# A perceiver layer on one core: FFN weight differences move from cross attention to self attention, and cross attention is reordered

## The reference, cut to what matters

```python
x = x + xattn(layernorm(x), ctx, Wq_d, W_qk, Wkv_d, Wv_u)       # 8 batches, 64 queries, 16 heads, 1601 context rows
x = x + attn(layernorm(x), ..., k_cache, v_cache, block_idx)     # 32 heads of 128, 8 key groups, 512 + 64 keys
x = x + ffn(layernorm(x), w1, mean_w1, w2, mean_w2, w3, mean_w3)

def xattn(Q, K, ...):
    C_kv = K @ Wkv_d                                             # 1601 x 32 per batch
    scores = ((Q @ Wq_d @ W_qk) per head) @ C_kv.T / sqrt(32)
    return softmax(scores) @ (C_kv @ Wv_u per head)

def weight(w, base):                                             # ffn: for w1, w3, w2
    d = w - base
    return base + mean(abs(d)) * sign(d)
h = silu(x @ W1.T) * (x @ W3.T);  y = h @ W2.T                   # inner size 1792
```

## Time and profile before

| | |
|---|---|
| three runs | 907.76, 906.02, 902.95 us; median 906.02 |
| profiled execution | 903.59 us, span 901.8 us |
| PE, DVE, ACT, POOL busy | 96%, 68%, 58%, 46% of the span |
| mean granted PE clock | 0.987 of full |
| cross attention | to 287 us (first score of batch 0 at 45 us) |
| keys and values of self attention | 287 to 316 us |
| heads of self attention | 316 to 764 us; grouped outputs begin 56.2 us apart (435.92, 492.15, 548.38) |
| output, norm and FFN | 764 to 902 us |
| ACT idle before exponentials of cross attention, ended by POOL's sums | 6.4 us in 3 waits |

### The profile page before, as it was taken

The page is one execution under the profiler, slowest core; times in us unless marked ns, Lnnn a source line. Parts: engine busy times, 40 slices in busy tenths (PEclk is TensorE's granted clock), DMA queues, the critical chain, the costliest instruction groups (busy, mean ns, idle before and its releaser), DMA issues.

```text
span 901.8 us, 15515 instructions
## 1 busy us (share of the span) xinstructions
PE 861.6 (96%) x5402; PEld 654.4 (73%) x5402; DVE 609.3 (68%) x994; ACT 521.6 (58%) x1011; POOL 416.4 (46%) x272
## 2 busy tenths in 40 slices
PE   6899999999987979999999999999999999899998
PEld 4445555555532768888888888888888887788886
DVE  4865676577543448768587685876858769767784
ACT  4756666666675546546365463654636557555552
POOL 2597787778874024423244232442324525144430
PEclk9989999999998989999999999999999999999999
DMA  9947756532651522011020110201102004446521
GB/s 358 325 169 273 275 209 213 192 127 66 217 174 59 222 83 71 24 41 54 0 70 23 43 50 0 70 23 40 53 0 70 13 1 137 144 141 204 188 99 47
DMA packets 43202, 102.96 MB, mean 114 GB/s; under 512 B 7954, under 2 KB 13074, under 8 KB 42258
## 3 DMA queue, kind: packets, MB, share of 16 engines
q1 hardware_dynamic: 42866, 102.06, 33.0%
q10 hardware_dynamic: 288, 0.26, 0.1%
HBM read 96.95 MB, written 1.05 MB: 109 GB/s over the span
## 4 chain that ended last, share of the span: by engine, by line
PE 61%; DVE 2%; ACT 1%; DMA 1%; POOL 0%; SPq 0%; issue 0%
PE psum L1359 11%; PE psum L1345 10%; PE psum L1475 9%; PE psum L1413 8%; PE psum L1371 6%; PE psum L1489 4%; PE psum L1398 3%; PE psum L1389 3%; PE psum L1394 3%; PE psum L1380 1%; PE psum L1392 1%; PE psum L1390 1%; DMA ffn_raw<-in_L_ffn_mean_w_dram 1%; POOL ffn_quant L1860 0%; DVE x L1831 0%; DVE norm_stats L162 0%
## 5 line engine op out<-in xcount | busy, mean ns | idle before, releaser
L1847 POOL TENSOR_TENSOR head_probs<-head_probs,inverse_den 128x576 f32<-128x576 f32 x128 | 147.4, 1152 | 273.1 <-DVE inverse_den L1700 273.0
L982 DVE TENSOR_REDUCE max_part<-psum 128x1 f32<-128x804 f32 x128 | 121.0, 989 | 44.0 <-PE psum L694 43.9
L871 ACT ACTIVATE probs<-psum 128x512 f32<-128x512 f32 (+1 forms) x208 | 107.9, 601 | 54.7 <-PE psum L715 48.1
L1582 ACT ACTIVATE head_probs<-psum,neg_max 128x576 f32<-128x576 f32 x128 | 94.8, 741 | 51.1 <-DVE neg_max L1713 50.4
L555 POOL TENSOR_TENSOR prob_sums<-probs 128x1024 f32<-128x1024 f32 x48 | 114.2, 2389 | 18.7 <-ACT probs L871 9.8
L1713 DVE TENSOR_REDUCE neg_max<-psum 128x1 f32<-128x576 f32 x128 | 96.9, 757 | 23.8 <-PE psum L1359 22.6
L1359 PE MATMUL psum<-k_high,query_t_high 128*128 (+1 forms) x256 | 86.6, 338 | 2.0 <-DVE coeff L1786 2.0
L1693 DVE TENSOR_TENSOR probs_t_low<-psum,probs_t_high 128x512 fp32r<-128x512 f32 x124 | 84.8, 684 | 1.0
L715 PE MATMUL psum<-q_t,c_t 97*128 97x512 f32 (+1 forms) x208 | 73.7, 435 | 7.9 <-ACT probs L871 6.3
L1371 PE MATMUL psum<-ident,head_probs 128*128 128x128 f32 x496 | 77.9, 273 | 1.6 <-DVE query_t_low L1672 1.4
L694 PEld LDWEIGHTS psum<-c_t,q_t 96*128 96x128 f32 x256 | 43.6, 190 | 47.9 <-DVE max_part L982 25.1
(11 more groups left out here) (221 smaller groups left out, 1919.3 us busy)
## 6 DMA issues: line engine op xcount, KB each, us to landing
ctx_t_odd<-in_ctx_dram SPq DMA_DIRECT2D x4, 3202.0 KB, 10.7
w_raw<-in_L_ffn_w_dram SPq DMA_DIRECT2D x24, 448.0 KB, 5.1
w_raw<-in_L_ffn_mean_w_dram SPq DMA_DIRECT2D x24, 448.0 KB, 6.4
ffn_raw<-in_L_ffn_w_dram SPq DMA_DIRECT2D x42, 256.0 KB, 3.8
ffn_raw<-in_L_ffn_mean_w_dram SPq DMA_DIRECT2D x42, 256.0 KB, 4.3
cache<-in_ctx_dram SPq DMA_DIRECT2D x3, 3202.0 KB, 10.8
wq_nat<-in_L_attn_wq_dram SPq DMA_DIRECT2D x32, 256.0 KB, 3.0
wo_nat<-in_L_attn_wo_dram SPq DMA_DIRECT2D x32, 256.0 KB, 2.7
```

The lines of the kernel that those rows point to most:

```text
L871: act.activation(prob_buffer(b, t)[0:rows, half * BANK:(half + 1) * BANK], psum[0:rows, n % SCORE_BANKS, :], ACT.Exp, scale=XSCALE).then_i ...
L982: dve.tensor_reduce(max_part[:, qt, pair:pair + 1], psum[:, bank:bank + 2, 0:PIECE_KEYS], AX.XY, ALU.max).then_inc(s_max, 1)
L1582: act.activation(probs[:, qt, :].rearrange("p (a k) -> p a k", a=2), psum[:, 2 * (qt % 2):2 * (qt % 2) + 2, 0:HALF], ACT.Exp, bias=neg_max ...
L1847: pool.tensor_tensor(probs[:, qt, :], probs[:, qt, :], rden[:, qt:qt + 1].to_broadcast([P, KEYS]), ALU.mult).then_inc(s["norm"], 1)
```

## The change

In `cross_attention`: the pieces of the FFN weights, their loads, differences and sums are taken out. The ring has 8 probability buffers. `values` takes two units at a visit, three visits a batch. POOL adds tiles into fewer sums (`GROUPED`): three for batches 0 to 4, five for 5 and 6, seven (two of them a single tile) for 7; tiles are added one by one, 10, 8 and 6 additions a batch (7 before). The values of the last, short tile go into the first pass of the denominators, and that function stands directly behind `turn_max`, ahead of `natural` and the next batch's first scores; before, the denominators stood behind those scores. Maxima and scores alternate one by one.

In `attention_and_ffn`: the pieces are 1024 wide, 7 of them, one per group from the second on. SP loads the three pairs (six DMAs of 512 KB) in its loop, after the wait for ACT's sum of the group before. POOL subtracts behind `values(g)` in the first head, ACT sums behind `output_weight_high(g, 0)`, POOL adds to the total in the second head. Two of the piece buffers lie over the selected keys, dead by then. The coefficient is made in the third head of the last group. `difference(0)` moves ahead of POOL's first head.

```diff
 def cross_attention
+STEADY = ((0, 1, 2, 3), (4, 5, 6, 7), (8, 9, 10, 11, 12))
+FEWER = ((0, 1, 2), (3, 4, 5), (6, 7), (8, 9), (10, 11, 12))
+FEWEST = ((0, 1, 2), (3, 4), (5, 6), (7, 8), (9, 10), (11,), (12,))
+GROUPED = (STEADY,) * (BATCH - 3) + (FEWER, FEWER, FEWEST)
+RING, SUMS = 8, 6
...
 max_scores, i == 1:
                     pe.wait_ge(s_d, 2 * (b - 1))
+                    if b + 1 < BATCH:
+                        pe.wait_ge(s_cnat, b + 2)
...
+            def tail_and_denominators(b):
...
                 if b + 3 < BATCH:
-                    pe.wait_ge(s_cnat, b + 4)
+                    pe.wait_ge(s_cp, b + 4)
                 elif b + 1 < BATCH:
                     pe.wait_ge(s_max, MAXIMA * (b + 2) - 1)
...
+                pe.wait_ge(s_exp, HALVES * (b + 1))
+                pe.wait_ge(s_add, adds_through(b, parts[0][-1]))
+                for half in range(2):
+                    at = 2 * LKV * half
+                    mm = pe.matmul(psum[at:at + LKV, U_BANK, :], c_nat[0:TAIL, b % 3, KT - 1, :],
+                                   prob_buffer(b, KT - 1)[0:TAIL, half * BANK:(half + 1) * BANK], start=False, stop=True)
+                    add_up(0, 1, half)
+                mm.then_inc(s_pv, 1)
+                for n in range(1, len(parts), 2):
+                    wait(pe, s_add, adds_through(b, parts[n + 1][-1]))
                     for half in range(2):
+                        add_up(n, 0, half)
+                        mm = add_up(n + 1, 1, half)
                 mm.then_inc(s_den, 1)
...
 PE's loop over batches:
+                maximum(0)
+                scores(b, 2)
+                if b == 0:
+                    maximum(1)
+                    compress(2)
+                scores(b, 3)
+                if b > 0:
+                    maximum(1)
+                    mix(b - 1)
+                maximum(2)
+                if b == 0:
+                    natural(2)
+                scores(b, 4)
+                maximum(3)
+                scores(b, 5)
+                maximum(4)
+                values(b, range(0, 2))
+                for t in range(6, 10):
+                    maximum(t - 1)
+                    scores(b, t)
+                maximum(9)
+                values(b, range(2, 4))
+                for t in range(10, KT):
+                    maximum(t)
+                    scores(b, t)
+                maximum(KT)
+                values(b, range(4, 6))
+                maximum(KT + 1)
+                maximum(KT + 2)
                 if b + 3 < BATCH:
                     compress(b + 3)
                 if lead:
                     turn_max(b + 1)
-                values(b, UNITS - 1)
+                tail_and_denominators(b)
                 if b + 3 < BATCH:
                     natural(b + 3)
                 if lead:
                     scores(b + 1, 0)
                     scores(b + 1, 1)
-                denominators(b)
...
 ACT's loop over batches:
-                    if t == ABS_AT:
-                        abs_sum(b, 0)
...
-                abs_sum(b, 1)
-                abs_sum(b, 2)
...
 attention_and_ffn, SP's loop:
+                    if i == 1:
+                        sp.wait_ge(s_abs, 3 * (g - 1) + 1)
+                        for k in range(3):
+                            for j, n in enumerate(wnames[k]):
+                                sp.dma_start(pieces[k][:, j, :], flat[n][:, bass.ds((g - 1) * PIECE, PIECE)]
+                                             ).then_inc(s_piece[k], 16)
...
 PE, score:
+                if isinstance(g, int) and n == NH - 2 and qt == 1:
+                    pe.wait_ge(s_tot, NKV)
+                    pe.matmul(psum[:, 3, HALF:HALF + 3], ones[:, :], total[:, :], start=True, stop=True).then_inc(s_all, 1)
+                elif isinstance(g, int) and n == NH - 2 and qt == 3:
+                    pe.wait_ge(s_co, 1)
...
 PE, start:
-            pe.wait_ge(s_ones, 1)
-            pe.wait_ge(s_tot, 1)
-            pe.matmul(psum[:, 7, 0:3], ones[:, :], total[:, :], start=True, stop=True).then_inc(s_all, 1)
-            pe.wait_ge(s_co, 1)
...
 ACT, head:
                 if this and i == 0:
                     output_weight_high(g, i)
+                if last and i == 0:
+                    for k in range(3):
+                        abs_sum(g, k)
+
+            def abs_sum(g, k):
+
+                if k == 0:
+                    act.wait_ge(s_tot, g)
+                act.wait_ge(s_pdiff, 3 * (g - 1) + k + 1)
+                act.activation(pieces[k][:, 0, :], pieces[k][:, 0, :], ACT.Abs,
+                               accum_out=part[:, k:k + 1]).then_inc(s_abs, 1)
...
 POOL, head:
+                if i == 1 and last and not (isinstance(g, int) and g == 0):
+                    pool.wait_ge(s_abs, 3 * g + 1)
+                    pool.tensor_tensor(total[:, :], total[:, :], part[:, :], ALU.add).then_inc(s_tot, 1)
                 if i == 0:
                     wait(pool, s["pv"], n)
                     values(g)
-                if isinstance(g, int) and (g, i) == (NKV - 1, 0):
-                    difference(0)
+                if i == 0 and last:
+                    pool.wait_ge(s["vl"], 2 * g + 2)
+                    for k in range(3):
+                        pool.wait_ge(s_piece[k], 32 * g)
+                        pool.tensor_tensor(pieces[k][:, 0, :], pieces[k][:, 0, :], pieces[k][:, 1, :],
+                                           ALU.subtract).then_inc(s_pdiff, 1)
...
 POOL, start:
+            pool.wait_ge(s["wql"], 2)
+            difference(0)
             run(pool, head)
```

More of the change, by code:

```diff
@@ L327, with adds_of, adds_before, adds_through @@
 C_WIDTH = MAIN + TAIL
-DIFF_AT = (0, 1, 2)
-ABS_AT = 3
+STEADY = ((0, 1, 2, 3), (4, 5, 6, 7), (8, 9, 10, 11, 12))
+FEWER = ((0, 1, 2), (3, 4, 5), (6, 7), (8, 9), (10, 11, 12))
+FEWEST = ((0, 1, 2), (3, 4), (5, 6), (7, 8), (9, 10), (11,), (12,))
+GROUPED = (STEADY,) * (BATCH - 3) + (FEWER, FEWER, FEWEST)
+def adds_of(b):
+    return [(t, n, t == tiles[1]) for n, tiles in enumerate(GROUPED[b]) for t in tiles[1:]]
+def adds_before(b):
+    return sum(len(adds_of(i)) for i in range(b))
+def adds_through(b, t):
+    done = [i + 1 for i, (at, n, first) in enumerate(adds_of(b)) if t == at or (first and t == GROUPED[b][n][0])]
+    return adds_before(b) + done[0] if done else 0
+def sum_number(b, n):
+    return sum(1 for i in range(b) for tiles in GROUPED[i] if len(tiles) > 1) + n
 COMPRESS_BANK = (4, 3, 6) + (4,) * (BATCH - 3)
@@ L440, in cross_attention, with tile_before, visits_done, tile_summed @@
     s_x = core.sem("x_updated", own)
-    wnames = (("w1", "mean_w1"), ("w3", "mean_w3"), ("w2", "mean_w2"))
-    flat = {n: arg[n].rearrange("r c -> (r c)").rearrange("(p f) -> p f", p=P) for pair in wnames for n in pair}
     def prob_buffer(b, t):
[L447 to L458, removed]
+        return probs[(KT * b + t) % RING]
+    def tile_before(b, t):
+        return divmod(KT * b + t - RING, KT)
+    def visits_done(b, t):
+        a, n = tile_before(b, t)
+        return VISITS * a + n // 4 + 1 if a >= 0 else 0
+    def tile_summed(b, t):
+        a, n = tile_before(b, t)
+        return adds_through(a, n) if a >= 0 else 0
+    def sum_buffer(b, n):
+        return sums[sum_number(b, n) % SUMS]
+    def sum_freed(b, n):
+        old = sum_number(b, n) - SUMS
+        return sum(1 for i in range(BATCH) if sum_number(i, 0) <= old)
     def query_copy(j, odd):
@@ L619, in _ @@
             pool.wait_ge(s_rest, 5)
[L620 to L623, removed]
-                    add_pair(s, u)
-                    if s == 0 and u == 0:
+            for b in range(BATCH):
+                for t, n, first in adds_of(b):
+                    add_tile(b, t, n, first)
+                    if b == 0 and t == 1:
                         compressed_low(2)
-                add_tail(s)
-                if s + 3 < BATCH:
-                    compressed_low(s + 3)
+                if b + 3 < BATCH:
+                    compressed_low(b + 3)
         @block.tensor
@@ L1264, in attention_and_ffn @@
     total = core.sb("abs_total", [P, 3], ctx=own)
+    part = core.sb("abs_part", [P, 3], ctx=own)
+    pieces = [over(f"w_piece{k}", [P, 2, PIECE], F32, "cache", 8 * k * PIECE) for k in range(2)]
+    pieces.append(core.sb("w_piece2", [P, 2, PIECE], ctx=own))
+    s_piece = [core.sem(f"w_piece_in{k}", own) for k in range(3)]
+    s_pdiff = core.sem("w_piece_diff_done", own)
+    s_abs = core.sem("w_piece_abs_done", own)
     coeff = core.sb("coeff", [P, 3], ctx=own)
```

137 lines of the change are left out of this document (48 added, 89 removed).

## The result

The changed kernel takes 940.66 us (median of four runs, 939.98 to 944.56) against 905.42 us before (four runs, 902.95 to 907.76): 1.040 times the time before, 95% interval 1.036 to 1.044. The forecast was 920 (907 to 930): the sign was right and the time lies 10.7 us above the range.

A forecast was written before the change was run, and what follows sets the result against it. PE was taken as the bound in both cross attention and self attention with FFN. Terms: 903.6 + 15.4 (sums) - 0.35 (coefficient) - 1.5 (cross attention) + 3 (clock) = 920 us, range 907 to 930.

The forecast's parts named there:

- The sums of |difference|: Self attention: ACT's three sums delay turned_high and PE's third turn by 2.2 us in each of seven groups, +15.4 us.
- The second rival: Self attention: the sums of |difference| hide, leaving only cross attention and the coefficient, 902 us; chance 0.12.
- The coefficient: Moved from before self attention's first score to beside PE work in the last group: together -0.35 us.
- The timetable of cross attention: New order walked by rows: 30.65 us a steady batch against 30.35, cross attention together -1.5 us.
- The clock: PE's granted clock falls to half behind new gaps: two falls taken, +3 us, bounds 0 and 15.
- the nine new gaps of 2.0 to 2.2 us: PE stalls of 2.2 us in seven self attention groups, and 2.0 us before the turn in batches 5 and 6.
- The evidence for that term: Cross attention before: half clock from 273.9 to 277.3, right behind 1.98 us idle, losing about 1.7 us.
- The third rival: Self attention: the clock falls in most gaps, 7 x 1.7 = 12 us over 917, giving 929 us; chance 0.18.
- the precedent: Cross attention before: the 1.98 us PE wait ended at 272.37, with a clock fall right behind it.
- The rule from the Trainium skill: PE's clock: its warning concerns idle gaps longer than those forecast, so no fall and a sum 3 us lower.

The follow-up runs named there:

- e2: Changed kernel with two of ACT's three sums of |difference| ahead of the first output weight's high part, the third after its second head, POOL's addition later: 921.8 us.
- e4: Changed kernel with the matmul of the first half of scores 3 issued five times in place of once in batches 1 to 7: 925.6 us.
- e5: Cross attention of the kernel before without differences and sums of FFN weights, with the changed kernel's self attention and FFN: 918.8 us.
- e1: Changed kernel with ACT's two copies of the denominators ahead of the exponentials of tile 0 in place of behind those of tile 1: 917.2 us.
- e6: Changed kernel with maxima 14 and 15 ahead of the values of tiles 8 to 11, nothing else: 935.9 us.
- e9: Changed kernel with ACT's two denominator copies split, one between exponentials of tiles 0 and 1, one between those of tiles 1 and 2: 947.7 us.
- e10: Kernel with denominator copies ahead of tile 0's exponentials (917.2 us), plus two spare ACT copies between exponentials of tiles 7 and 8, batches 1 to 7: 927.2 us.
- e8: Kernel before with two more ACT copies to a spare buffer ahead of each batch's copies of the denominators: 914.7 us.
- e11: Kernel before with four spare ACT copies ahead of each batch's copies of the denominators: 938.1 us.

## Why the prediction was wrong

- **The sums of |difference|.** Right. 15.4 us forecast from a stall of 2.2 us in each of seven groups; 2.06 each, 14.4 measured, and e2 takes them away. The second rival (902) fell.
- **The coefficient.** Right as far as it shows: -0.35 forecast, and the wait before the first score went from 1.97 to 1.41 us. The stretch it is in is 0.7 us shorter, but that stretch takes 34.7 us in e4 and 37.8 in e5 with the same coefficient code, so the time does not measure it.
- **The timetable of cross attention.** Right for the steady batch: 30.65 us was forecast and 30.8 is what e4 shows where the clock holds. Its cross attention as a whole is 4.7 us over before, forecast -1.5. From first score to first score, e4 against before: up to batch 1 +0.8 (forecast -0.9), batches 1 to 4 +1.9 (+1.2), batches 5 and 6 +6.5 (+2.9), the last -4.5 (-4.7). In each of batches 5 and 6 a fall of 3.4 us (at 229.5 and 260.3) follows the wait for the turn, 1.83 us where 2.0 was forecast; at the prices measured here the two are worth some 3 us of the miss. Up to batch 1 a wait of 0.77 us for POOL's sums before the denominators of batch 0 was not forecast; the rest there stays open.
- **The clock, the step that failed.** The prediction said that "the nine new gaps of 2.0 to 2.2 us can do this, but the work around most of them is denser", took two falls at 1.7 us, 3 us in all, with an upper bound of 15. Three things in it were wrong. Of the nine gaps (2.06 us seven times, 1.83 twice) one brought a fall; the falls came at the gaps of 1.36 us in each batch, which are not among the nine. A fall in these batches was not 3.4 us long but 6.8 or 10.2, and cost a batch 2.3 to 3.3 us. And there was one in every batch. Measured against e4: 17.0 us in cross attention, and 1.7 by the prediction's own price for the fall at 650 us, in place of 3, so that even the bound of 15 was passed. The profiled execution lies 940.25 - 920 = 20.3 us over the forecast: 15.7 are this term, 6.2 the timetable as e4 shows it, -1.0 the sums, and -0.6 the start and what is left over.
- **The evidence for that term** was read too narrowly. The kernel before had not one fall behind a gap of some 2 us but four: also at 287.6, 318.3 and 325.1 us, at waits of 2.42, 2.38 and 1.97 us. These were all its waits of 1.9 us or more from 60 us on, and each brought a fall; this spoke for more than two of nine, and that only one of them came is luck. Two rows of it, PE's timeline and the windows:

```profile
318.11 1.86 PE L1345 MATMUL psum<-attn_x_high,wq_t_high 128*128 128x512 f32 x4 [2.38 <-DVE wq_t_low L1668]
```

```profile
325.20:328.50 3.30, 3.30 (x14) 3.06 (x14) 1.49 (x3) 0.83 (x2) 0.00 (x0) 0.50 0.02 5
```

- **The third rival** (929) had the mechanism, a clock that falls because a fixed period repeats, but put it into self attention, where PE's work is dense, and at 1.7 us each. Its premise, that a gap longer than the precedent brings a fall, is refuted by six of seven here. But the share is not fixed: the same gap in the same self attention brought a fall in 11 of 49 places over seven kernels (the changed one 1 of 7, e1 1, e4 2, e5 3, e6 1, e9 2, e10 1).
- **The rule from the Trainium skill** ("TensorE: Matmul & The Clock Gate", "Why this matters for your kernels"), by which no gap here was long enough for a fall, would have given 917. The measurement decides against it: gaps of 1.36 us, and of 0.23 and 0.62 us together, were enough. Another section of that page of the Trainium skill, "A second HAM failure mode: psum-queue depth-cycling", tells of a kernel in which frequent short idle times of PE between groups of matmuls made the clock go up and down. e9 agrees with that, with 65.8 us of half clock and no wait over 0.73 us in a steady batch.

What stays open is why the new order falls with 1.58 us of idle PE (0.22 and 1.36) in each batch where the old one, with 1.74 (0.22 and 1.52, with the denominators' 2.8 us of matmuls between), falls in three of six. That the idle time lies closer together in the new order, and behind lighter work, would fit both, and e9 and e10; no run changed that alone. It can't be the whole: e8's batches 1 to 5 are alike, and two of them fall, and the wait of 1.83 us before a turn brought a fall within 1 us in e4, both times, and none in the changed kernel. The moment at which a wait comes may count beside its surroundings; no run moved a wait in time and left the rest as it was.

## What to carry to other kernels

Price a PE wait in a loop at its length plus the chance of a clock fall behind it, and don't take that chance from the longest gap alone: cutting one wait in two (e9) made it worse. In the trace before, look for every fall and the wait ahead of it, and count the waits of that length without a fall too. Where a wait can't be removed, either move what causes it to where the engine that causes it is idle (e1, e2: a few lines each, worth some 23 and 19 us), or give PE something to do in it (e4). To see what the clock costs, compare the same group of matmuls at two places of one batch, 3.64 against 1.92 us here.

## What the hardware showed that I had not expected

PE with 28 useless matmuls more ran the kernel 15 us faster. A microsecond at half clock cost 0.37 us of time in the new order (e4 against the changed kernel) and 0.43 in the old (e11 against before), less than the 0.5 that the prediction took. And in e9, with a fall in every batch, the batches came 34.0 to 34.2 us apart up to the fifth, and the falls began at 116.6, 150.8, 184.9, 219.0 and 253.2 us; where the clock holds (e4) a batch of the changed order takes 30.8.
